# A reordered tail and second round in a graph-attention kernel on one core

## What is computed

```
h = maximum(layernorm(x), 0)
hi_t = (h @ W1[:384])[:, :, None, :] + dep_emb @ W1[384:] + b1
hj_t = (h @ W2[:384])[:, None, :, :] + dep_emb @ W2[384:] + b2
relevance = sum(hi_t * hj_t, axis=-1)
A = softmax(where(adj != 0, relevance, -1e9), axis=2)
z = relu((A @ h) @ gcn_w + gcn_b)
out = x + z @ Wo + bo
```

## Time and profile before

| | us |
|---|---|
| median of 3 runs | 360.76 (360.28 to 360.89) |
| the profiled execution's own time | 359.88 |
| its span, first to last instruction | 358.1 |
| TensorE busy | 346.7 (97%) |
| VectorE busy | 264.7 (74%) |
| ScalarE busy | 264.9 (74%) |
| GpSimd busy | 175.2 (49%) |

### The profile page before, as it was taken

One profiled execution on the slowest core, in us unless ns is written; L12 is line 12 of the kernel. 1 busy time (PEld: TensorE's weight loads), 2 busy tenths in 40 slices (PEclk: granted clock), 3 DMA queues, 4 the chain that ended last, 5 costly groups with the idle time before them and its releaser, 6 DMA issues.

```text
span 358.1 us, 9301 instructions
## 1 busy us (share of the span) xinstructions
PE 346.7 (97%) x3068; PEld 213.7 (60%) x3068; DVE 264.7 (74%) x664; ACT 264.9 (74%) x563; POOL 175.2 (49%) x354
## 2 busy tenths in 40 slices
PE   7999999899999999999999999999999999999985
PEld 6766565565657566565656566565756566565753
DVE  0998788686968777785968777695967777586664
ACT  2399896977787977778797877778697877755642
POOL 3067573756637182745638183745628183770000
PEclk9999999999999999999999999999999999999999
DMA  7994608965859395775759395675749383645052
GB/s 230 320 209 141 179 2 176 236 140 120 207 126 231 89 262 119 191 173 121 203 117 249 88 255 125 174 176 128 201 109 266 88 205 90 160 91 154 11 165 100
DMA packets 97000, 57.54 MB, mean 161 GB/s; under 512 B 60450, under 2 KB 96932, under 8 KB 96980
## 3 DMA queue, kind: packets, MB, share of 16 engines
q1 hardware_dynamic: 96272, 56.90, 63.8%
q10 hardware_dynamic: 644, 0.20, 0.3%
q0 software_dynamic: 64, 0.20, 0.2%
HBM read 17.44 MB, written 12.58 MB: 84 GB/s over the span
## 4 chain that ended last, share of the span: by engine, by line
PE 87%; DVE 4%; ACT 4%; DMA 2%; issue 1%; DVEq 0%; SPq 0%; ACTq 0%
PE bank L1174 24%; PE bank L1175 24%; PE bank L1176 24%; PE bank L1428 3%; PE bank L1423 3%; PE bank L1277 3%; PE bank L1285 2%; DMA x_all<-in_L_gnn_W_w_dram 2%; PE bank L1218 2%; ACT bank L652 1%; ACT h_tok L497 1%; PE bank L1488 1%; PE bank L1490 1%; ACT h_parts L497 1%; DVE bank L1069 0%
## 5 line engine op out<-in xcount | busy, mean ns | idle before, releaser
L449 POOL TENSOR_TENSOR h_parts<-h_tok,h_parts 128x1536 f16<-128x1536 f32 (+1 forms) x15 | 43.6, 2907 | 94.4 <-ACT h_parts L497 94.3
L1174 PE MATMUL bank<-gw_hi,hT 128*128 128x385 f16 x192 | 63.1, 328 | 1.6 <-DVE g_parts L924 1.1
L1176 PE MATMUL bank<-gw_hi,hT 128*128 128x385 f16 x192 | 62.7, 327 | 0.0
L425 POOL TENSOR_TENSOR x_all<-x_all,bo_all 128x1536 f32 (+1 forms) x16 | 55.0, 3442 | 15.7 <-ACT h_tok L515 15.7
L1175 PE MATMUL bank<-gw_lo,hT 128*128 128x385 f16 x192 | 62.6, 326 | 0.0
L924 DVE TENSOR_TENSOR g_parts<-bank,g_parts 128x512 f16<-128x512 f32 x48 | 33.2, 691 | 36.0 <-ACT bank L570 35.8
L1174 PE MATMUL bank<-wo_hi,z_hi 128*128 128x384 f16 x180 | 58.9, 327 | 0.5 <-DVE z_lo L1044 0.5
L1176 PE MATMUL bank<-wo_hi,z_lo 128*128 128x384 f16 x180 | 58.7, 326 | 0.0
L1175 PE MATMUL bank<-wo_lo,z_hi 128*128 128x384 f16 x180 | 58.7, 326 | 0.0
L1174 PE MATMUL bank<-hT,m_hi 128*128 128x512 f16 x144 | 54.6, 379 | 0.7 <-DVE hT L747 0.7
L1175 PE MATMUL bank<-hT,m_hi 128*128 128x512 f16 x144 | 54.6, 379 | 0.0
(11 more groups left out here) (165 smaller groups left out, 644.2 us busy)
## 6 DMA issues: line engine op xcount, KB each, us to landing
x_all<-in_x_dram SPq DMA_DIRECT2D x16, 768.0 KB, 6.9
out_dram<-x_all SPq DMA_DIRECT2D x15, 768.0 KB, 5.2
hg_parts<-hg_lo SPq DMA_DIRECT2D x32, 192.0 KB, 3.6
hg_parts<-hg_hi SPq DMA_DIRECT2D x32, 192.0 KB, 3.9
x_all<-in_L_gnn_W_w_dram SPq DMA_DIRECT2D x2, 576.0 KB, 5.2
out_dram<-x_all SPq DMA_DIRECT2D x4, 192.0 KB, 1.9
gcn_raw<-in_L_gnn_gcn_w_dram SPq DMA_DIRECT2D x1, 576.0 KB, 10.8
x_all<-in_L_gnn_Wo_w_dram SPq DMA_DIRECT2D x1, 576.0 KB, 11.5
```

The costliest lines, as they stand in the source:

```text
L425: nc.gpsimd.tensor_tensor(x_all[:, s, :, :], x_all[:, s, :, :], bo_all[:, :, :].broadcast_to([P, KT, D]), ALU.add).then_inc(x_biased, 1)
L449: ins = nc.gpsimd.tensor_tensor(h_parts[:, at, 1, :], h_tok[:, at, :], h_parts[:, at, 0, :], ALU.subtract)
L1174: nc.tensor.matmul(dst, lh, rh, start=(c == 0), stop=False)
L1176: last = nc.tensor.matmul(dst, ll, rh, start=False, stop=(c == DC - 1))
```

## The change

In five places, nothing that is computed on all rounds is added or dropped:

1. Round 1, ScalarE: the three high parts of Wo come behind the three high parts of h(1) and the first moved score half, where one stood ahead of them.
2. Round 1, ScalarE: the first high part of hg(1) stands between the high part and the whole of z's first chunk; the others of hg(1) are behind z and behind the first moved score half, and each waits for its row term.
3. Round 1, VectorE: the last low part of Wo goes ahead of the statistics of x(3), the row term and low part of hg's tile 0 ahead of z's low parts, the other row terms between z's low parts, and the masks and sums ahead of the other low parts of hg. Row terms wait for the product itself (`hg_done`), not for the high part.
4. Round 1, TensorE: the first output product of round 0 waits for z's low part chunk by chunk (`z_split` of e + 1), where all three chunks were waited for at once.
5. Round 15: TensorE makes the scores ahead of hg's tile 3. VectorE makes three masks with a row term and a fourth without, and adds tile 3's row term to the sums afterwards (one more instruction on 128x64). The low parts of hg tiles 2 and 3 go behind the exponentials' bias. The transposes of the last attention stand ahead of the last of four output tiles. The last aggregation does the moved parts of each chunk first and waits for attention's high copy after them. SP moves the last hg in six DMAs in place of four: low parts of tiles 0 and 1, high parts of all tiles, low parts of tiles 2 and 3, each with its own wait.

The core of the diff:

```diff
+            def move_last_hg():
+
+                def move_part(lanes, part, tiles):
+                    for g in range(GT):
+                        sp.dma_start(hg_parts[lanes, tiles, g, :], part[g * S:(g + 1) * S, tiles, :])                          .then_inc(hg_moved, 16)
+
+                sp.wait_ge(z_done, DC * LAST)
+                sp.wait_ge(hg_split, KT * LAST + 2)
+                move_part(slice(0, S), hg_lo, slice(0, 2))
+                sp.wait_ge(hg_high, KT * (LAST + 1))
+                move_part(slice(S, 2 * S), hg_hi, slice(0, KT))
+                sp.wait_ge(hg_split, KT * (LAST + 1))
+                move_part(slice(0, S), hg_lo, slice(2, KT))
...
+                    if c == 2 and last:
+
+                        act.wait_ge(row_ready, KT * s + DC)
                     hg_high_part(s, c)
-                hg_high_part(s, DC)
+                if not last:
+                    hg_high_part(s, DC)
...
             def second_round():
-                wo_high_part(0)
                 for c in range(DC):
                     early_high_part(1, c)
                 move_scores(0, range(1))
-                wo_high_part(1)
-                wo_high_part(2)
+                for c in range(DC):
+                    wo_high_part(c)
...
-                z_parts(0, 0, bank[Z_BANK[0]][:, :])
+                z_high_part(0, 0, bank[Z_BANK[0]][:, :])
                 act.wait_ge(z_done, DC)
                 hg_high_part(1, 0)
-                z_parts(0, 1, bank[Z_BANK[1]][:, :])
-                z_parts(0, 2, bank[Z_BANK[2]][:, :])
+                z_whole(0, bank[Z_BANK[0]][:, :])
+                for c in range(1, DC):
+                    z_parts(0, c, bank[Z_BANK[c]][:, :])
+                move_scores(1, range(1))
                 for k in range(1, KT):
+                    act.wait_ge(row_ready, KT + k + 1)
                     hg_high_part(1, k)
-                move_scores(1)
+                move_scores(1, range(1, GT))
                 exponentials(1)
                 normalise(3)
...
+                if isinstance(s, int) and s == LAST:
+
+                    act.wait_ge(row_ready, KT * NSUP)
+                    hg_high_part(s, DC)
...
+            def last_masks():
+
+                dve.wait_ge(row_ready, KT * LAST + DC)
+                for k in range(DC):
+                    nc.vector.tensor_scalar(masks[:, k, :], bias_all[:, KT * LAST + k, :], row_term[:, k:k + 1],
+                                            None, ALU.add).then_inc(masked, 1)
+                nc.vector.tensor_copy(masks[:, DC, :], bias_all[:, KT * LAST + DC, :]).then_inc(masked, 1)
+
+            def last_row():
+
+                dve.wait_ge(hg_done, KT * NSUP)
+                row_of(LAST, DC)
+                dve.wait_ge(row_ready, KT * NSUP)
+                dve.wait_ge(scored, LAST + 1)
+                nc.vector.tensor_scalar(scores[:, DC, :], scores[:, DC, :], row_term[:, DC:DC + 1], None,
+                                        ALU.add).then_inc(scored, 1)
+
+            def masked_scores(s, last=False):
+                if not last:
+                    all_masks(s)
...
+            def score_maxima(s, last=False):
                 dve.wait_ge(summed, GT * (s + 1))
                 dve.wait_ge(score_copied, GT * (s + 1))
                 nc.vector.tensor_tensor(scores[:, :, :], scores[:, :, :], score_moved[:, :, :],
                                         ALU.add).then_inc(scored, 1)
-                dve.wait_ge(scored, s + 1)
+                if last:
+                    last_row()
+                dve.wait_ge(scored, s + 2 if last else s + 1)
...
+                wo_low_part(2)
                 part_statistics(3, range(KT))
-                z_low_part(0, 0, bank[Z_BANK[0]][:, :])
                 rows_and_low(1, 0)
-                z_low_part(0, 1, bank[Z_BANK[1]][:, :])
-                wo_low_part(2)
-                z_low_part(0, 2, bank[Z_BANK[2]][:, :])
-                for k in range(1, KT):
-                    rows_and_low(1, k)
+                for c in range(DC):
+                    z_low_part(0, c, bank[Z_BANK[c]][:, :])
+                    dve.wait_ge(hg_done, KT + c + 2)
+                    row_of(1, c + 1)
                 dve.wait_ge(bias_made, 2)
-                scored_and_added(1)
+                all_masks(1)
+                summed_scores(1)
+                for k in range(1, DC):
+                    hg_low_part(1, k)
+                score_maxima(1)
+                hg_low_part(1, DC)
+                add_output(0, range(2))
+                attention(1)
+                add_output(0, range(2, KT))
...
+                    if c == 2 and isinstance(s, int) and s == LAST:
+                        last_aggregated()
+                        return
...
+            def last_aggregated():
+
+                dve.wait_ge(hg_done, KT * LAST + DC)
+                row_of(LAST, 2)
+                last_masks()
+                z_low_part(LAST - 1, 2, bank[Z_BANK[2]][:, :])
+                masked_scores(LAST, last=True)
+                hg_low_part(LAST, 2)
+                hg_low_part(LAST, DC)
+                add_output(LAST - 1, range(1))
+                attention(LAST)
+                add_output(LAST - 1, range(1, 2))
...
             attention_high(2)
+            add_output(LAST - 1, range(2, KT))
             for c in range(DC):
...
+            def last_aggregation():
+
+                pe.wait_ge(attT_copied, 2)
+                hg_read(KT * NSUP)
+                pe.wait_ge(score_copied, GT * NSUP)
+                pe.wait_ge(summed, GT * NSUP)
+                pe.wait_ge(hg_moved, MOVES * LAST + 16 * 3 * GT)
+                for c in range(DC):
+                    for k in range(KT):
+                        for g in range(GT):
+                            at = k * P + g * S
+                            nc.tensor.matmul(bank[LAST_Z_BANK[c]][:, at:at + S], hg_parts[:, k, g, c * P:(c + 1) * P],
+                                             attT_parts[:, k, g, :], start=(k == 0 and g == 0), stop=False,
+                                             skip_group_check=True)
+                    pe.wait_ge(attT_high, GT * 2)
+                    for k in range(KT):
+                        last = nc.tensor.matmul(bank[LAST_Z_BANK[c]][:, k * P:(k + 1) * P],
+                                                hg_hi[:, k, c * P:(c + 1) * P], attT_hi[:, k, :, :], start=False,
+                                                stop=True, skip_group_check=True)
+                    last.then_inc(z_done, 1)
...
+            def z_ready(c):
+                pe.wait_ge(z_split, c + 1)
+
             def output(s):
-                pe.wait_ge(z_split, DC * s)
+                first = isinstance(s, int) and s == 1
+                if not first:
+                    pe.wait_ge(z_split, DC * s)
                 for k in range(KT):
                     rows = slice(k * P, (k + 1) * P)
+                    if k == DC and isinstance(s, int) and s == LAST:
+                        transposed_attention(LAST + 1)
                     if k == DC:
 
                         hg_read(KT * s + DC)
                     split_product(bank[O_BANK[k]][:, 0:D],
                                   lambda e: (z_hi[:, e, rows], z_lo[:, e, rows]),
-                                  lambda e: (wo_hi[:, e, :], wo_lo[:, e, :])).then_inc(o_done, 1)
+                                  lambda e: (wo_hi[:, e, :], wo_lo[:, e, :]),
+                                  z_ready if first and k == 0 else None).then_inc(o_done, 1)
...
+                last = isinstance(s, int) and s == LAST
                 for k in range(KT):
+                    if last and k == DC:
+                        scored_supertile(s, half)
                     free_hg_tile(s, k, half)
                     if k == 0:
                         aggregation(s, Z_BANK)
-                scored_supertile(s, half)
+                if not last:
+                    scored_supertile(s, half)
                 output(s)
...
-            transposed_attention(LAST + 1)
-            aggregation(LAST + 1, LAST_Z_BANK)
+            last_aggregation()
```

More of the change, by code:

```diff
@@ L327, in _ @@
                     transpose_h(s + 2, s % 2)
-                move_hg(s + 1)
                 if s + 1 < LAST:
+                    move_hg(s + 1)
                     transpose_attention(s + 1)
+                else:
+                    move_last_hg()
                 store_out(s)
@@ L573, in z_parts, with z_high_part @@
             def z_parts(s, c, z_bank):
+                z_high_part(s, c, z_bank)
+                z_whole(c, z_bank)
+            def z_high_part(s, c, z_bank):
                 act.wait_ge(z_done, DC * s + c + 1)
@@ L1060, in masked_scores, with summed_scores @@
                                             None, ALU.add).then_inc(masked, 1)
+            def last_masks():
[14 more added lines that the diff above has]
+                    all_masks(s)
+                summed_scores(s)
```

(12 more changed lines are left out.)

7 lines of the change are left out of this document (5 added, 2 removed).

## The result

The changed kernel takes **358.03 us**, median of 6 runs (357.86 to 359.13), beside 360.27 (360.20 to 360.89, 6 runs) for the kernel before: ratio 0.9937, 95% interval 0.9923 to 0.9951. That is 0.6% or 2.2 us faster. 359.2 was forecast, and the lower end of the range was 358.4. The profiled execution takes 357.86.

What follows compares the result with a forecast made beforehand. TensorE, busy 97%, was taken as the bound, so only its waits could be saved: 0.23 at round 2's head plus 1.30 at the end, 1.53 us, taken from a median of 360.76, gives 359.2; range 358.4 to 360.3.

Steps and rivals of the forecast that it cites:

- The median: Whole kernel: median of the runs taken as 0.88 us above the profiled execution, turning 359.88 into 360.76 before the gain.
- The chain to the last store is the same: After the last aggregation: same 36 matmuls, then z and output, up to the last store; no change in time.
- The end: Round 15 and after: maxima 1.41 earlier, wait of 1.32 covered, last aggregation at 345.74 instead of 347.04; gain 1.30 us.
- from exponentials to the attention's low part: At the end: exponentials go from 341.91 to 340.50, attention's low part from 344.83 to 343.42, distance kept.
- from the transposes to the next matmul: At the end, TensorE: the transposes take 0.37 before the last nine output matmuls run.
- Rivals 3 and 4: 3 (0.11): last hg moves land late, 360.2 with 1 us; 4 (0.08): maxima come forward by only half, 359.9.
- Wo's high parts: Round 1, ScalarE: moved behind h(1)'s high parts, they bring everything up to the first attention's transposes 0.52 earlier.
- Wo's last low part: Round 1, VectorE: waits for GpSimd's subtraction, takes 1.8 to 1.9 instead of 0.61, ends 0.4 behind it.
- Rivals 1 and 2: 1 (0.20): Wo step never waits for GpSimd, exponentials 0.6 to 0.9 earlier; 2 (0.06): GpSimd keeps port, 361.6.
- The exponentials of round 1: Round 1, ScalarE: start at 58.4 instead of 58.62, so the head of round 2 gains 0.23 us.
- the power step: Round 1, GpSimd: 1.01 us step, taken to make VectorE's masks wait 0.2.
- the two low parts of hg between the sums: Round 1, VectorE: two of 0.46 between masks and sum of halves, 0.92 less 0.1 for a wait they fill.

Runs made afterwards that it cites:

- e7: Kernel before, with three tiny memsets that run on VectorE between rounds 14 and 15, shifting its later instructions by three places; 359.38 us, ratio 0.9990.
- e13: Changed kernel, without three VectorE memsets in a branch that is never entered, so later instructions stand three places earlier in its list; 358.28 us.
- e14: Kernel before, with three more VectorE memsets in a branch that is never entered, so later instructions stand three places further on; 360.10 us.
- e9: Changed kernel, with the last attention's transposes put back behind the fourth output tile; 358.84 us.
- e10: Changed kernel, with the last hg moves as in the kernel before, four DMAs behind the last low part of hg; 359.97 us, ratio 1.0007.
- e12: Changed kernel, with TensorE's scores of round 15 back behind hg's tile 3, other engines keeping their new order; 359.48 us.
- e5: Changed kernel, with one added wait: GpSimd's first subtraction of round 1 starts only when Wo's last low part is done; 357.62 us.

## Why the prediction was wrong

359.2 was 1.2 us too slow, and the time fell below the range. Two terms made it so: the 0.88 added for the median, of which 0.17 was there, and, in the mechanism, the chain behind the last aggregation, which I took to be unchanged and which became 0.39 shorter. The difference is the sum of the following terms.

**The median, 0.71.** I added 0.88 to the profiled execution because the median of three runs stood that far above it. Later medians of the same kernel, of 15 to 23 runs, are 359.82 to 359.95, at most 0.07 above the profiled one, and after's is 0.17 above its own. With 0.17 in place of 0.88 the forecast would have been 358.5. This is the largest term of the miss, and has nothing to do with the change. The gain itself was 1.53 by my sum, 1.96 by the traces.

**"The chain to the last store is the same", 0.39.** The step of the mechanism that failed. The order of that chain is the same, but three more instructions ahead of it shift VectorE's list, and the pause goes (e7, e13, e14). VectorE's idle time of 1.53 ahead of the first addition stood in the trace of before, and I did not ask how much of it the three matmuls explain.

**The end, 1.30 against 1.56.** Rows of VectorE in after, for the earlier trace rows, and ScalarE's exponentials:

```profile
339.70 0.42 DVE L1140 TENSOR_REDUCE row_max<-bank 128x4 f32<-128x256 f32 x1
...
343.25 0.42 DVE L1166 SCALAR_TENSOR_TENSOR att_all<-bank,att_all 128x256 f16<-128x256 f32 x1
```

```profile
340.43 0.38 ACT L674 ACTIVATE bank<-bank,exp_bias,exp_scale 128x64 f32<-128x64 f32 x1 [0.57 <-DVE exp_bias L1142]
```

The mechanism held step by step: the output starts at 338.86, the maxima start 0.84 behind it (forecast 0.87), the exponentials 1.57 (1.59), transposes with a short wait, none ahead of the last aggregation. Two terms were too large: from exponentials to the attention's low part 2.82, not the 2.92 of the earlier trace rows; from the transposes to the next matmul 0.23 (343.73 to 343.96), not 0.37, since the next product does not wait for their end. e9, e10 and e12 show that scores, transposes and moves all carry it. Rivals 3 and 4 fall.

**Wo's high parts, 0.52 against 0.35.** ScalarE does start earlier, 36.10, but now it waits for the transposes to end, and VectorE follows 0.77 behind it where it was 0.61; why it follows later no run tests. The two rows of after, of ScalarE and VectorE, beside the earlier trace rows:

```profile
36.10 1.58 ACT L536 ACTIVATE hT<-bank 128x512 f16<-128x512 f32 x3 [0.77 <-PE bank L1297]
```

```profile
36.87 1.89 DVE L780 SCALAR_TENSOR_TENSOR hT<-bank,hT 128x512 f16<-128x512 f32 x3 [0.59 <-ACT hT L536]
```

**Wo's last low part.** Right, and shown by e5: 1.75, TensorE's wait 1.34 at tile 3 (forecast 1.4), none at the output. Rivals 1 and 2 fall. In e5, where the step does not wait, the exponentials come 0.41 earlier than before (24.66 against 25.07), so rival 1 was priced too high with 0.6 to 0.9.

**The exponentials of round 1, 0.23 against 0.01.** 0.17 is the missing part of Wo's high parts. Inside the chain two errors cancelled: the power step did not hold the masks (0.2 less), and the two low parts of hg between the sums took 1.05, not 0.82 (0.23 more). That the head of round 2 follows the exponentials was right in every row of the table: the two columns move together to 0.02.

Together: 0.71 + 0.39 + 0.26 - 0.22 + 0.05 for the first weight is 1.19, the miss of 1.2.

## What to carry to other kernels

A move that hides a step beside another engine's work must be paid against what that engine is doing just then: Wo's last low part cost 1.75 in the gap where it seemed free, and e5's one wait on the engine with time to spare gave back 0.40. At the end of this kernel the last handovers of the engines had to come early together: scores, transposes and moves each undo about half of the gain or more when one alone goes back. And a constant offset between two traces of an unchanged chain is worth a look at the place of its instructions in the list: three instructions that never run moved a pause of 0.39.

## What the runs showed of the hardware

- With the last additions at number 452 of its list VectorE paused for 0.39 us, and a block of instructions was fetched 0.7 to 0.9 behind the first addition's start; at number 455 there was no pause (16 traces).
- A GpSimd step on 128x4 elements that took 1.04 did not hold back four masks of VectorE (0.74), while its addition of 128x1536 did.
- The two traces of before agree to 0.01 us in every column of the table. What moves between traces is the landing of the first weight: the row that waits for it stands at 7.49 (e10) to 8.57 us (e13), and the traced execution of e13, with 8.57, took 359.14 beside a median of 358.28.
